# Third cross-attention of a Perceiver kernel: the symmetric key sums in four column tiles of 32, with block rows of 130, 98, 66 and 34 columns, in place of two of 64

## The reference, cut to what matters

```python
H, D, DIM = (8, 128, 256)
f_q, f_k, f_v = (proj(q), proj(k), proj(v))      # layer norm, then 256 -> 8 heads x 128; k and v are the same keys
dots = jnp.einsum('hqnd,hqmd->hqnm', f_q, f_k)
qn = jnp.linalg.norm(f_q, axis=-1)
kn = jnp.linalg.norm(f_k, axis=-1)
cosine_sim = dots / (qn[..., :, None] * kn[..., None, :])
...
var_component = jnp.einsum('hqn,hqm->hqnm', q_ratio, k_ratio)
...
mixed = cw * cosine_sim + vw * cov_component + ww * var_component
out = jnp.einsum('hqnm,hqmd->hqnd', mixed, f_v)
```

## Time and profile before

| | |
|---|---|
| Median of 3 runs | 2570.8 us (2569.28 to 2570.88) |
| The profiled execution's own time | 2571.34 us |
| Its span in the trace | 2569.6 us |
| PE busy over the span | 90% |
| DVE, ACT, POOL busy | 71%, 46%, 20% |
| Mean granted clock of PE | 0.94 of full speed |
| The stage `l2_xattn` in the trace | about 1461 to 1977 us |

### The profile page before, as it was taken

How to read it: one execution, slowest core, us unless ns; L and a number is a source line. 1 busy time by engine, 2 the same in 40 slices (tenths; PEclk the granted TensorE clock), 3 DMA queues, 4 the chain that set the end, 5 groups by cost and what they waited for, 6 DMA issues and landing times. The chain is left out here.

```text
span 2569.6 us, 57124 instructions
## 1 busy us (share of the span) xinstructions
PE 2310.1 (90%) x21794; PEld 1419.9 (55%) x21794; DVE 1831.9 (71%) x2832; ACT 1194.1 (46%) x2049; POOL 520.7 (20%) x300
## 2 busy tenths in 40 slices
PE   3999989999996969999996999999997559999979
PEld 2444436666665836656665746665556415555548
DVE  6888778889886266666634388888886777777721
ACT  4566553333335337777772333333332426556552
POOL 0555440000000030000001055555662010000000
PEclk7999989999997969999997999999998669999989
DMA  8577755656645567666734422222212366676644
GB/s 275 200 245 247 264 181 143 197 164 173 183 148 189 192 160 172 161 159 162 169 79 149 163 101 100 100 100 100 79 70 53 101 131 151 158 161 152 149 139 171
DMA packets 245951, 397.62 MB, mean 155 GB/s; under 512 B 28921, under 2 KB 210304, under 8 KB 245668
## 3 DMA queue, kind: packets, MB, share of 16 engines
q1 hardware_dynamic: 240132, 393.90, 53.6%
q10 hardware_dynamic: 5664, 1.44, 0.3%
HBM read 316.44 MB, written 78.06 MB: 154 GB/s over the span
## 5 line engine op out<-in xcount | busy, mean ns | idle before, releaser
L1640 DVE CUSTOM_DVE_ANT_0 l3x_junk<-l3x_pm,l3x_mrow,l3x_top 128x896 bf16<-128x896 f32 x224 | 246.1, 1148 | 84.0 <-PE l3x_pm L1796 83.5
L1724 ACT ACTIVATE l1x_prob<-l1x_ring,mask_col 128x512 f32<-128x512 f32 x392 | 247.9, 684 | 115.9 <-PE l1x_ring L1816 114.7
L1727 ACT ACTIVATE l3x_prob<-l3x_ring 128x512 f32<-128x512 f32 x392 | 213.1, 595 | 161.1 <-PE l3x_ring L1820 161.1
L1174 ACT ACTIVATE l0x_att_pt<-l0x_att_pt 128x1024 f32<-128x1024 f32 x99 | 104.7, 1057 | 253.8 <-DVE l0x_att_pt L1109 253.8
L2804 POOL TENSOR_TENSOR l2x_gk<-l2x_f,first_vin 128x1024 f32<-128x1024 f32 x98 | 184.3, 1916 | 160.7 <-DVEq L2545 160.7
L1219 PE MATMUL l0x_att_pv<-l0x_wv,l0x_att_vin 128*128 128x512 f32 x392 | 196.0, 623 | 0.0
L2678 PE MATMUL l2x_kf<-l2w_w,l2x_nin 128*128 128x512 f32 x392 | 173.1, 601 | 4.6 <-DVE l2x_f L2519 4.5
L2678 PE MATMUL l2x_kf<-l2w_w,l2w_first 128*128 128x512 f32 x392 | 170.3, 594 | 0.0
L2519 DVE SCALAR_TENSOR_TENSOR l2x_f<-l2x_kf,l2x_rs,l2w_bias 128x1024 f32<-128x1024 f32 x98 | 125.8, 1283 | 55.3 <-PE l2x_kf L2678 43.0
L1640 DVE CUSTOM_DVE_ANT_0 l1x_junk<-l1x_pm,l1x_mrow,l1x_top 128x896 bf16<-128x896 f32 x112 | 123.7, 1148 | 56.6 <-PE l1x_pm L1796 56.6
L1640 DVE CUSTOM_DVE_ANT_0 l1x_junk<-l1x_pm,first_mrow,l1x_top 128x896 bf16<-128x896 f32 x112 | 123.4, 1147 | 49.8 <-PE l1x_pm L1796 49.8
(11 more groups left out here) (730 smaller groups left out, 4924.2 us busy)
## 6 DMA issues: line engine op xcount, KB each, us to landing
first_kt<-scratch_KS SPq DMA_DIRECT2D x84, 448.0 KB, 9.2
scratch_KT<-l0x_max_kf SPq DMA_DIRECT2D x28, 896.0 KB, 4.8
l0x_att_kt<-scratch_KT SPq DMA_DIRECT2D x56, 448.0 KB, 7.0
scratch_KS<-l0x_side_kp SPq DMA_DIRECT2D x14, 1344.0 KB, 13.5
l1x_kt<-scratch_KS SPq DMA_DIRECT2D x42, 448.0 KB, 9.6
scratch_KS<-first_kt SPq DMA_DIRECT2D x14, 1344.0 KB, 5.9
l3x_kt<-scratch_KS SPq DMA_DIRECT2D x42, 448.0 KB, 9.0
l0fw_w<-L_ffn_exp_w SPq DMA_DIRECT2D x16, 1024.0 KB, 7.7
```

Source lines behind the costliest of these rows:

```text
L1640: dve.tensor_tensor_reduce(junk[x % 2][:, :, :], pm[x % 2][:, :, 0:SPLIT], mrow[b][:, :].rearrange("p (s k) -> p s k", s=2), 1.0, top[1 - ...
L1724: ins = act.activation(into, scores, ACT.Exp, bias=R.mask_col[:, bass.ds(m * TILES + n // 4, 1)])
L1727: ins = act.activation(into, scores, ACT.Exp)
```

## The change

The 128 features of a head are cut in four parts of 32 (r = 0 to 3) in place of two of 64. Block row r has weights of 32 features and takes the last 130 - 32r columns of `gk`: 130, 98, 66, 34. The array then works as four column tiles, which write to PSUM partitions 0 to 31, 32 to 63, 64 to 95 and 96 to 127. Eight heads are two groups of four; in a group the four heads n of one r are called behind each other, head n into column tile (r + n) % 4, so that from one r to the next the order of the tiles turns by one place.

At the stage's end the copies are regrouped by r: DVE copies r = 0 and 1, ACT r = 2 and 3, each copy takes 32 partitions of two heads. There are three off-diagonal blocks per head to be turned in place of one: 24 transposes, into `pc` and the free `pf[1]`, then three copies on DVE and two on ACT, and "M" counts to 2. The core of the diff (the functions `width`, `sums_at` and `turned_at` only give places):

```diff
-            def matrix_parts(h):
-
-                pair, g = h // 2, h % 2
-                return ((Msb[0:HALF, h, :], pM[64 * g:64 * g + 64, pair // 2, upper(pair)]),
-                        (Msb[HALF:HD, h, HALF:], pM[64 * (1 - g):64 * (1 - g) + 64, pair // 2, lower(pair)]))
+            def width(r):
+
+                return GW - 32 * r
...
+            def matrix_parts(r):
+
+                for n in range(4):
+                    have = slice(32 * ((r + n) % 4), 32 * ((r + n) % 4) + 32)
+                    first = 2 * width(r - 1) if r % 2 else 0
+                    yield (Msb[32 * r:32 * r + 32, n:H:4, 32 * r:],
+                           pM[have, r // 2, first:first + 2 * width(r)].rearrange("p (a n) -> p a n", a=2))
...
                     dve.wait_ge(S.sem("M_turned"), 1)
-                    dve.tensor_copy(Msb[HALF:HD, :, 0:HALF], pc[0:HALF, :].rearrange("p (h d) -> p h d", h=H)).then_inc(
-                        S.sem("M"), 1)
+                    dve.tensor_copy(Msb[64:96, :, 0:64], pc[0:32, :].rearrange("p (h d) -> p h d", h=H))
+                    dve.tensor_copy(Msb[96:P, 5:H, 0:96], pf[1][0:32, 1, 0:288].rearrange("p (h d) -> p h d", d=96))
+                    dve.tensor_copy(Msb[32:64, 0:7, 0:32], pf[1][0:32, 1, 288:512].rearrange(
+                        "p (h d) -> p h d", d=32)).then_inc(S.sem("M"), 1)
...
+                    act.wait_ge(S.sem("M_turned"), 1)
+                    act.activation(Msb[96:P, 0:5, 0:96], pf[1][0:32, 0, 0:480].rearrange("p (h d) -> p h d", d=96), ACT.Copy)
+                    act.activation(Msb[32:64, 7, 0:32], pf[1][0:32, 0, 480:512], ACT.Copy).then_inc(S.sem("M"), 1)
...
-                            for pair in range(H // 2):
-                                for g in range(2):
-                                    h = 2 * pair + g
-                                    last = pe.matmul(pM[64 * g:64 * g + 64, pair // 2, upper(pair)],
-                                                     f[b][:, t, h * HD:h * HD + HALF], gk[b][:, t, h, :],
-                                                     start=False, stop=False, skip_group_check=True)
...
+                            for group in range(2):
+                                for r in range(4):
+                                    bank, at = sums_at(r, group)
+                                    for n in range(4):
+                                        h, to = 4 * group + n, 32 * ((r + n) % 4)
+                                        last = pe.matmul(pM[to:to + 32, bank, at],
+                                                         f[b][:, t, h * HD + 32 * r:h * HD + 32 * r + 32],
+                                                         gk[b][:, t, h, 32 * r:], start=False, stop=False,
+                                                         skip_group_check=True)
...
-                    for h in range(H):
-                        last = pe.transpose(pc[0:HALF, h * HALF:(h + 1) * HALF], Msb[0:HALF, h, HALF:HD],
-                                            R.ident[0:HALF, 0:HALF])
+                    pe.wait_ge(S.sem("fqT"), 1)
+                    for r in range(1, 4):
+                        for h in range(H):
+                            last = pe.transpose(turned_at(r, h), Msb[0:32 * r, h, 32 * r:32 * r + 32],
+                                                R.ident[0:32 * r, 0:32 * r])
```

More of the change, by code:

```diff
@@ L2422, in use, with sums_at, turned_at @@
                 return k % 2, i * TILES + k // 2
[L2424 to L2432, removed]
-            def matrix_parts(h):
-                pair, g = h // 2, h % 2
-                return ((Msb[0:HALF, h, :], pM[64 * g:64 * g + 64, pair // 2, upper(pair)]),
-                        (Msb[HALF:HD, h, HALF:], pM[64 * (1 - g):64 * (1 - g) + 64, pair // 2, lower(pair)]))
+            def width(r):
+                return GW - 32 * r
+            def sums_at(r, group):
+                first = 2 * width(r - 1) if r % 2 else 0
+                return r // 2, slice(first + group * width(r), first + (group + 1) * width(r))
+            def matrix_parts(r):
+                for n in range(4):
+                    have = slice(32 * ((r + n) % 4), 32 * ((r + n) % 4) + 32)
+                    first = 2 * width(r - 1) if r % 2 else 0
+                    yield (Msb[32 * r:32 * r + 32, n:H:4, 32 * r:],
+                           pM[have, r // 2, first:first + 2 * width(r)].rearrange("p (a n) -> p a n", a=2))
+            def turned_at(r, h):
+                if r == 1:
+                    return pf[1][0:32, 1, 288 + 32 * h:320 + 32 * h] if h < 7 else pf[1][0:32, 0, 480:512]
+                if r == 2:
+                    return pc[0:32, 64 * h:64 * h + 64]
+                return pf[1][0:32, 0, 96 * h:96 * h + 96] if h < 5 else pf[1][0:32, 1, 96 * (h - 5):96 * (h - 4)]
             def seen(h):
@@ L2567, in _ @@
                     after(dve, S.counted("f_used1"), steps)
-                    for h in range(H // 2):
-                        for to, have in matrix_parts(h):
+                    for r in range(2):
+                        for to, have in matrix_parts(r):
                             last = dve.tensor_copy(to, have)
@@ L2645, in _ @@
                     after(act, S.counted("f_used1"), steps)
-                    for h in range(H // 2, H):
-                        for to, have in matrix_parts(h):
+                    for r in range(2, 4):
+                        for to, have in matrix_parts(r):
                             last = act.activation(to, have, ACT.Copy)
                     last.then_inc(S.sem("M_copied"), 1)
+                    act.wait_ge(S.sem("M_turned"), 1)
+                    act.activation(Msb[96:P, 0:5, 0:96], pf[1][0:32, 0, 0:480].rearrange("p (h d) -> p h d", d=96), ACT.Copy)
+                    act.activation(Msb[32:64, 7, 0:32], pf[1][0:32, 0, 480:512], ACT.Copy).then_inc(S.sem("M"), 1)
                     norm_scalar(act, S, "h", nw3, rows=H)
@@ L2755, in _ @@
                     pe.wait_ge(S.sem("late_loads"), late.total)
-                    pe.wait_ge(S.sem("M"), 1)
+                    pe.wait_ge(S.sem("M"), 2)
                     pe.wait_ge(S.sem("corr_sq"), 1)
```

5 lines of the change are left out of this document (removed).

## The result

The changed kernel takes 2651.2 us (median of 4 runs, 2650.1 to 2654.3), the kernel before on the same chip 2570.0 us (2568.7 to 2570.9). The ratio is 1.032, 95% interval 1.031 to 1.033: slower by 81 us, where 14 us less were forecast. The profiled execution has a span of 2648.7 us.

A forecast was written before the change was run, and what follows sets the result against it. PE was taken to set the pace of the key loop. 2571.3 us, less 16.7 for 91 faster tiles of keys, plus 1.9 at the stage's end, gave 2556.5; forecast 2556.0 us, range 2550 to 2567.

The forecast's parts named there:

- 12 gathers of 1.29 us: Key loop: each gather of seven tiles becomes 1.29 us shorter, at 0.184 us a tile of keys.
- Rival 1: Pace of passes: each round of four takes 0.11 us whatever its columns, 1.76 us a tile; +39 us, 2610; chance 0.10.
- Against it: Head of the loop: PE's sequencer passes four calls at most 30 ns each, where 1.17 us for 32 wants 37.
- The loop after the change: Gathers: columns 1102 ns plus spacing 38 ns; 1.17 us a tile of keys taken, bounds 1.140 and 1.20, before 1.354.
- short burst of l3x_O: Four matmuls within 0.05 us speak against a pass floor across column tiles, not against one in feeding instructions.
- break-even of 21.1 ns: Gathers: spacing per pass at which 64 passes take the 1.354 us a tile of before.
- overhead of about 60 cycles a matmul: Counterargument from pages: with starts about 25 ns apart at least, 64 passes take 1.6 us; time near 2595.
- Rival 2: Weight loads share a path: 34-column rounds take 55 ns, +0.106 us a tile; -5.2 us, 2565.6; chance 0.14.
- turned order: Gathers: strictly ordered calls start each round one place late, 0.056 us a tile of keys; about half taken.
- DVE's cover: Turn of the loop: DVE's smallest reserve, 1.68 us, covers gathers 1.29 us shorter, leaving 0.2 to 0.4 us.
- stage's end: After the last gather: DVE's copies +1.1 us, last copies +0.84 us; together +1.9, up to +2.9 if transposes outlast DVE's work.

The follow-up runs named there:

- kernel with 96 calls fewer: Changed kernel without the second group of heads in three tiles of every looped gather, 408 calls a turn, sums partly missing: 2549.3 us, ratio 0.992.
- sorted one: Against the kernel before: block rows of 130, 98 and 66 columns, each gather's 32-row calls first, then its 64-row calls: 2569.3 us, ratio 1.000.
- straight code: Kernel before with PE's key loop written out in full, no branch, same calls and waits: 2569.8 us, ratio 1.000.
- split kernels: Changed kernel, loop written out, each gather cut into pieces between parts of the projection: two pieces 2593.7 us, three pieces 2591.2 us.

## Why the prediction was wrong

**Where the 95 us are.** The loop from its first instruction to the last branch took 79.8 us longer in the trace after (496.3 and 416.5 us), where 12 gathers of 1.29 us were to make it 15.5 shorter: the whole miss of 95 us lies there. A turn by its parts: two projections of 24.23 us and two gathers of 7 x 1.137 + 0.14 = 8.10 us would be 64.7 us; the forecast had 65.1. The trace has 81.8. Of the 17.1 us between, PE stands still in 11.8 (3.45 and 3.90 in the gathers, 4.41 at the branch), and most of the rest is the half clock behind these three standstills, 2.5 to 3.4 us of work each: the 189 passes behind the first take 5.13 us, at a mean clock of 0.69, where at full clock they and the change would be 3.5. From the first branch to the last, five turns, it is 409.0 us where 325.6 were forecast, 83.4 more; the first turn, which stalls in its gathers alone, brings the other 11.8.

**The step that failed** is the argument against Rival 1 ("Against it: at the head of the loop PE's sequencer gets past four calls ... at most 30 ns a call"). It took a burst of four calls at the head of a loop whose code was loaded for a price that lasts, and it asked only for the pace of calls, never for their code. "The loop after the change" counted columns and spacing and left out that 504 calls are 2,016 instructions where 280 were 1,120. The prediction itself said of the short burst of l3x_O that it does not speak against a floor in the feeding of instructions, and then put no time on it; no rival had the code of the loop. In its place the runs showed code that is fetched anew in every turn: 11.8 us a turn of standing still, and the clock that falls behind it. The kernel with 96 calls fewer has neither behind its first turn. The rows to see it were there: the page of before has a queue of instruction blocks, with 123 packets and none inside the loop, and the counts of the earlier trace rows give the calls of a turn. They would have shown that the loop lived on code that stays, but not at which size that ends.

**Rival 1 as written** forecast the right side for another reason, even distances of the passes and 10 us or more a gather, and its 2610 us are 41 short. The gather did get longer, 13.54 us, but not evenly: four tiles run at 1.137 us, and then nothing runs. The pace of passes itself, 1.137 us for 64, 17.8 ns a pass, is below its break-even of 21.1 ns and lasts as long as there is code. The overhead of about 60 cycles a matmul (the Trainium skill, TensorEngine Tiling (Array Packing), Instruction Overhead), taken as a floor on the pace, stood in the prediction beside an estimate of 1.6 us a tile of keys. The 1.137 us do not agree with such a floor across column tiles.

**Rival 2** is refuted by the same number: 1.137 us leaves no room for 0.106 us of shared weight loads. The turned order cost nothing either: 1.140 was the bound without it, against the 1.17 that I took.

**DVE's cover.** In the kernel with 96 calls fewer and in the sorted one PE never waits for DVE inside the loop, in the former at a turn of 61.7 us, shorter than the 65.1 of the forecast. With full calls in a loaded loop it could not be tried, since that loop is too large.

**The stage's end** came as worked out: copies 3.21 us against 3.14, last copies 0.68 + 0.45 + 0.38 against 684 + 455 + 389 ns, DVE waiting 0.98 us for the transposes where up to 1 us was the bound: +2.9 us, the upper end of what I gave.

The Trainium skill (Runtime: NRT & Kernel Launch, Instruction fetch mechanics) says that PE's instruction memory holds 2048 instructions and is refilled in blocks of 16 KiB by a DMA queue of its own, that crossing a block is mostly hidden, and that a taken branch stalls until its target is fetched if that is outside a window of two blocks. The size of a block and the stall at the branch agree with the rows (16 KiB; 4.5 us against 0.21). The window of two blocks does not: at some 64 calls a block, the loop of 408 calls spans over six, and its branch took 0.21 us. The 2048 instructions were not reached either: 1,760 did not stay. That crossings are mostly hidden holds for the calls of before (straight code 2569.8 us) and not for the changed ones.

**What stays open**: when each block is asked for, and so why pieces of 96 calls still stall. That the stalls hang on queue 8 is in the packets: each of the 12 gathers of the changed loop goes on 2.2 to 2.5 us after a packet has started, and the shorter stalls of the split kernels 2.2 to 2.9 us after one. But the queue was not busy ahead of them. Between 1597 and 1606 it starts no packet, though PE works on the gather from 1599.81 and stands still at 1604.77; the one that ends the stall starts at 1606.02. So the first stall of a gather is a block that comes late, not a block that takes 3.5 us, and a comparison of calls per block with 3.5 us is an argument that no run here proves. The bound between 408 and 440 calls was not narrowed.

## What to carry to other kernels

Before splitting a matmul into more and smaller ones in a hardware loop, count PE's instructions in the body (four for each f32 call here) and look at the instruction queue in the stretch: a body without fetches is a resource, and this one held 1,632 instructions and not 1,760. A short burst proves the pace of an engine, not that its code arrives at that pace; a split that halves a call's time doubles its demand for code. And what a loaded loop wins must still pay for the first turn and for straight code: there bursts of 64 of the dense calls with projections between them ran through, and most of those of 96 and more stood still, for 0.2 to 4.6 us. A standstill can cost more than itself: behind each of those of 3.3 us and more in the changed loop the clock was at half for some 3 us, while behind 0.70 us in the split kernel it stayed at 1.00. Last, an order that gives the fetch time can uncover a wait elsewhere, here 4.2 us for the norms.

## What the runs showed of the hardware

- Four column tiles of 32 run wholly side by side, down to passes of 34 columns: 1.137 us for 64 passes whose columns alone, at 0.84 ns, are 1.102.
- A change between calls of 32 and of 64 rows costs about 0.14 us of PE (tile 1.54 us, by columns and spacing 1.25).
- PE's code of a loop stays loaded at 1,632 instructions and some waits and not at 1,760.
- A loop whose code doesn't stay pays 3.7 to 4.8 us a taken branch in place of 0.21, and past the threshold its size matters little: 2647.0, 2646.2 and 2651.2 us for 440, 472 and 504 calls a turn, after 2549.3 for 408.
- Behind each of the 17 standstills of the changed loop, 3.3 to 4.7 us long, the granted clock was 0.50 for some 3 us; behind stalls of 0.50 and 0.70 us in the split kernel it was 1.00.
- No kernel here that computes the whole result beat the one before: its two column tiles of 64 need the fewest calls, and at 85 ns a call (1.354 us for 16) they fit both the loop and the fetch.
